# Recurrent step of a two-layer kernel: the fp32 products of update gate and candidate move from VectorE to GpSimd, and the candidate's tanh to SBUF

## Chip, cores and metric

One core of a Trainium2 chip (trn2). The metric is the device time of one execution in microseconds (us); the runs of the kernel before have a median of 7208.16 us.

## The reference, cut to what matters

Layer 0 (a gated transform of x by a small network on `cond`) is cheap here. Layer 1 is a gated recurrent unit over 2048 steps, with batch 2 and width 512, and its steps depend on each other:

```
def step(h, xs):
    xzt, xrt, xht = xs
    z = jax.nn.sigmoid(xzt + h @ U_z + vz)
    r = jax.nn.sigmoid(xrt + h @ U_r + vr)
    hh = jnp.tanh(xht + r * h @ U + vh)
    h_new = (1.0 - z) * h + z * hh
    return (h_new, h_new)
```

The kernel returns x plus these outputs. The products of x with W_z, W_r and W don't depend on h.

## The kernel before, in words

**Layout.** The width of 512 is K = 4 chunks of P = 128 partitions; batch is B = 2, so a state tile is 128 x 8 (S = 8) and half of it is 128 x 4 (HS = 4). Each fp32 factor of a product with U is split in two fp16 parts (PARTS = 2). `h_part` holds for each chunk four fp16 parts: high and low of the kept share (1-z)h and high and low of the new share z*hh. `rh_part` holds the two parts of r*h.

**One step on TensorE** (`steps`, L270, products in `tile_product`, L261). It waits for `hs0` and runs the first 16 matmuls of the reset gate into `pair_r` (input chunks 0 and 1), waits for `hs1` and runs the other 16 (chunks 2 and 3). Then 32 matmuls of the update gate into `ps_z`, and 32 of the candidate into `pair_h`, after `rh0` and `rh1`. The candidate comes in two halves, each with its own PSUM bank. After it, in four of five steps, a piece of the next block's input projection runs (`ps_p`, L238), which doesn't depend on h.

**VectorE** (`step`, L498) sums the parts of each product (`total`, L495), builds r*h (L504, L508, L513), the kept share (L532, L533, L537) and the new share. The new share has three operations per half: `new_high` (L542) rounds z_mul times tanh to fp16 in `h_part`; `new_full` (L546) computes the same product in fp32 as `zn`; `new_low` (L551) subtracts the one from the other and increments `hs0` or `hs1`. L563 then adds `keep` and `zn` to `h_cur`.

**ScalarE** does the tanh of each sum (L359), the copies that turn tanh into z_keep and z_mul (L376, L377), and the seeds: copies of the precomputed input share `xp` into the PSUM banks as one more addend (L342, L345). The tanh of the candidate's halves is written into its own bank in PSUM. Before it seeds `pair_h`, ScalarE waits for `zn1`, as `new_full` reads that bank.

**GpSimd** has only the setup (L188 to L200), and no instruction in the steps.

**Order.** Each engine runs its instructions in the order written; the engines are tied by semaphores, written out by hand, which count to the number of the step. The 2048 steps are 32 blocks of 64. A block begins with four steps with extra work (`turn`: transposes of x and of the output), then come 12 rounds of five steps with a projection each.

**Lines that matter**: the order of the tail of a step on VectorE (L554 to L563), L380 to L382 on ScalarE, L278 (the wait for `hs0` and `hs1`) on TensorE.

Of the kernel before, what the change touches and what calls it, by code (L numbers as in the profile page):

```python
# [1 line left out]

# [3 lines left out]
ALU = mybir.AluOpType  # L24
# [7 lines left out]
P = 128  # L32
R, Z, H = 0, 1, 2
# [4 lines left out]
def gru_kernel(nc, x, cond, W1, b1, W2, b2, W_z, U_z, C_z, b_z, W_r, U_r, C_r, b_r, W, U, C, b, out):  # L38
    B, T, D = x.shape
    K = D // P  # L40
    S = K * B
    HC = K // 2
    HS = S // 2
# [16 lines left out]
    with ExitStack() as ctx:  # L60
        def sb(name, shape, dt=F32):
            return ctx.enter_context(nc.sbuf_tensor(name, shape, dt))
# [43 lines left out]
        keep = sb("keep", [P, S])  # L106
        z_mul = sb("z_mul", [P, S])
        zn = sb("zn", [P, S])

# [3 lines left out]
        ps_r, ps_h = ([pair[:, hf, :] for hf in range(2)] for pair in (pair_r, pair_h))  # L115
        SUM, TANH = 64, 96

        def cols(bank, g, m0, m1):
# [6 lines left out]
                 "v_mm v_raw_ok v_ok umax_ok uall_ok upow scale_ok uhi u_ok w_ok "  # L125
                 "x_in x_tr y_ok y_copied proj0_mm proj0_ok wst_in proj_mm o_sum o_tr o_ev out_st "
                 "seed0 h0_ready r0_mm r1_mm z_mm z_keep h_ok h0_mm h1_mm r0_sum r1_sum z_sum h0_sum h1_sum r0_th r1_th z_th h0_th h1_th "
                 "rh32_0 rh32_1 rh0 rh1 keep_ok zn0 zn1 hs0 hs1 copied")
        s = {n: ctx.enter_context(nc.semaphore("s_" + n)) for n in names.split()}
        block = ctx.enter_context(nc.Block())  # L130

# [1 line left out]
        kb = lambda a: a.rearrange("p (k b) -> p k b", b=B)  # L133
        UG, WG, CG = (U_r, U_z, U), (W_r, W_z, W), (C_r, C_z, C)
        half = (slice(0, HS), slice(HS, S))
# [50 lines left out]
        @block.gpsimd  # L186
        def _(pool):
            nc.gpsimd.memset(ident[:, :], 0.0).then_inc(s["ident_zero"], 1)  # L188
            pool.wait_ge(s["ident_zero"], 1)
            nc.gpsimd.affine_select(out=ident[:, :], in_=ident[:, :], compare_op=ALU.not_equal, fill=1.0,  # L190
                                    base=0, pattern=[[-1, P]], channel_multiplier=1).then_inc(s["ident_ok"], 1)

            nc.gpsimd.memset(h_cur[:, :], 0.0)
            nc.gpsimd.memset(hist[:, TB:2 * TB, :], 0.0)
            nc.gpsimd.memset(y_cur[:, :, :], 0.0)
            nc.gpsimd.memset(h_part[:, 0:HC], 0.0).then_inc(s["hs0"], 1)
            nc.gpsimd.memset(h_part[:, HC:K], 0.0).then_inc(s["hs1"], 1)
            nc.gpsimd.memset(xp[:, :, TB:2 * TB, :], 0.0).then_inc(s["h0_ready"], 1)
            pool.wait_ge(s["umax_ok"], G)
            nc.gpsimd.partition_all_reduce(u_all[:, :], u_max[:, :], P, RMAX).then_inc(s["uall_ok"], 1)  # L200

        @block.tensor
        def _(pe):
# [123 lines left out]
        @block.scalar  # L327
        def _(act):
            A = nc.scalar.activation
            act.sem_inc(s["out_st"], BYTES)  # L330
            for n, nm in enumerate(("mlp1", "mlp2")):
                act.wait_ge(s[nm + "_pre"], 1)
                A(mlp_tanh[:, n, :], mlp_pre[:, n, :], ACT.Tanh, scale=0.5).then_inc(s[nm + "_th"], 1)
            act.wait_ge(s["scale_ok"], 1)
            for g in range(G):
                A(u_part[:, g, 0], u_raw[:, g], ACT.Copy, scale=u_scale[:, g:g + 1]).then_inc(s["uhi"], 1)

            def seed(banks, g, at):

                src = xp[:, g * K:(g + 1) * K, at, :]  # L340
                if g == Z:
                    return A(cols(banks, Z, 0, K)[:, :, ADDENDS[Z] - 1, :], src, ACT.Copy)  # L342
                a = ADDENDS[g]
                to = banks[:, :, 0:a * HS].rearrange("p h (m a b) -> p h m a b", a=a, b=B)
                return A(to[:, :, :, a - 1, :], src.rearrange("p (h m) b -> p h m b", h=2), ACT.Copy)  # L345

            act.wait_ge(s["h0_ready"], 1)
            act.wait_ge(s["proj0_ok"], 2 * G)
            for g, banks in ((R, pair_r), (Z, ps_z), (H, pair_h)):
                seed(banks, g, 0).then_inc(s["seed0"], 1)  # L350


            scale_reg = [act.alloc_register(f"tanh_scale_{g}") for g in range(G)]
            for g in range(G):
                act.reg_load(scale_reg[g], tanh_scale[0:1, g:g + 1].bitcast(I32))

            def tanh(to, bank, g, n, wait, t1, done):
                act.wait_ge(s[wait], t1)
                A(to, bank[:, SUM:SUM + n], ACT.Tanh, scale=scale_reg[g]).then_inc(s[done], 1)  # L359

            def steps(t0, count, ring, turn=None):

                for u in range(count):
                    t1 = act.snap(t0 + (u + 1))

                    prv = act.snap(ring + (u - 1) if u else (ring + (2 * TB - 1)) % (2 * TB))
                    nxt = act.snap(ring + (u + 1) if u < count - 1 else (ring + count) % (2 * TB))
                    for hf in range(2):
                        tanh(ps_r[hf][:, TANH:TANH + HS], ps_r[hf], R, HS, f"r{hf}_sum", t1, f"r{hf}_th")

                    A(hist[:, prv, :], h_cur[:, :], ACT.Copy)  # L371
                    tanh(th_z[:, :], ps_z, Z, S, "z_sum", t1, "z_th")

                    seed(pair_r, R, nxt)
                    act.wait_ge(s["z_th"], t1)
                    A(z_keep[:, :], th_z[:, :], ACT.Copy, scale=-0.5, bias=0.5).then_inc(s["z_keep"], 1)  # L376
                    A(z_mul[:, :], th_z[:, :], ACT.Copy, scale=H_SCALE / 2, bias=H_SCALE / 2)  # L377
                    tanh(ps_h[0][:, TANH:TANH + HS], ps_h[0], H, HS, "h0_sum", t1, "h0_th")
                    seed(ps_z, Z, nxt)
                    tanh(ps_h[1][:, TANH:TANH + HS], ps_h[1], H, HS, "h1_sum", t1, "h1_th")  # L380
                    act.wait_ge(s["zn1"], t1)
                    seed(pair_h, H, nxt)  # L382
                    if turn is not None and u == 1:
                        act.wait_ge(s["o_sum"], turn)
                        A(y_cur[:, :, :], y_next[:, :, :], ACT.Copy).then_inc(s["y_copied"], 1)
                    if turn is not None and u == 2:
                        put_out(turn)

            def put_out(nb):
                act.wait_ge(s["o_tr"], nb)  # L390
                act.wait_ge(s["out_st"], nb * BYTES if isinstance(nb, int) else act.snap(nb * BYTES))
                A(o_tok[:, :], ps_o[:, :], ACT.Copy).then_inc(s["o_ev"], 1)

            with act.Fori(0, NB) as n:
                steps(act.snap(n * TB), TURN, act.snap((n % 2) * TB), act.snap(n + 1))
                with act.Fori(0, GM) as i:
                    steps(act.snap(n * TB + i * BODY + TURN), BODY, act.snap((n % 2) * TB + i * BODY + TURN))
            act.wait_ge(s["h_ok"], T)
            A(hist[:, (T - 1) % (2 * TB), :], h_cur[:, :], ACT.Copy).then_inc(s["copied"], 1)
            put_out(NB + 1)  # L400

        @block.vector
        def _(dve):
            V = nc.vector
# [93 lines left out]
            def step(t1):  # L498
# [41 lines left out]
                def new_high(hf):  # L540
                    dve.wait_ge(s[f"h{hf}_th"], t1)
                    V.tensor_tensor(h_part[:, kc[hf], NEW, :], kb(z_mul[:, half[hf]]),  # L542
                                    kb(ps_h[hf][:, TANH:TANH + HS]), ALU.mult)

                def new_full(hf):
                    V.tensor_tensor(zn[:, half[hf]], z_mul[:, half[hf]], ps_h[hf][:, TANH:TANH + HS],  # L546
                                    ALU.mult).then_inc(s[f"zn{hf}"], 1)

                def new_low(hf):
                    dve.wait_ge(s[f"zn{hf}"], t1)  # L550
                    V.tensor_tensor(h_part[:, kc[hf], NEW + 1, :], kb(zn[:, half[hf]]), h_part[:, kc[hf], NEW, :],  # L551
                                    ALU.subtract).then_inc(s[f"hs{hf}"], 1)

                new_high(0)  # L554
                dve.wait_ge(s["h1_mm"], t1)
                total(ps_h[1], H, HC, "h1_sum")
                new_full(0)
                keep_low()
                new_low(0)
                new_high(1)  # L560
                new_full(1)
                new_low(1)
                V.tensor_tensor(h_cur[:, :], keep[:, :], zn[:, :], ALU.add).then_inc(s["h_ok"], 1)  # L563

# [12 lines left out]
            def steps(t0, count, proj=None, turn=None):  # L577


                for u in range(count):  # L580
                    step(dve.snap(t0 + (u + 1)))
                    if proj is not None and u == K - 1:
                        store_projection(*proj)
                    if turn is not None and u == 0:

                        make_out(turn[0])
                    if turn is not None and u == 2:
                        dve.wait_ge(s["y_copied"], turn[1])
                        make_y(turn[2])
# [35 lines left out]
```

## Time and profile before

| | |
|---|---|
| runs, median (lowest to highest) | 7208.16 us (7206.21 to 7209.48), 3 runs |
| profiled execution, span from first to last instruction | 7205.8 us |
| setup, to the first step | 74.5 us |
| busy share PE, DVE, ACT, POOL | 94%, 74%, 46%, 0% |
| instructions PE, DVE, ACT, POOL | 200232, 43503, 22603, 13 |
| granted TensorE clock, mean | 0.502 |

The profile gives the span of its execution and no separate time beside it. PE is TensorE's matmuls, PEld its weight loads, DVE is VectorE, ACT ScalarE, POOL GpSimd. The ends of matmuls are modelled, so a row of 32 matmuls may reach past the start of the next row: what counts is the distance of starts. In a timeline a row holds the start in us from the beginning of the span, the duration in us, engine, line, operation, result and operands, and the count of instructions; what stands in brackets is the idle time of the engine ahead of it and what ended it. The row of a VectorE or ScalarE operation is longer than the distance to the next independent one on its engine: they overlap.

### The profile page before, as it was taken

How to read it: one execution, taken by the hardware profiler on the slowest of the kernel's cores; microseconds unless marked ns; L12 is line 12 of the kernel's file. 1: busy time of each engine (PE TensorE's matmuls, PEld its weight loads, DVE VectorE, ACT ScalarE, POOL GpSimd, SP SyncE). 2: the span in 40 equal slices, each digit the busy share in tenths (PEclk: the TensorE clock that was granted, in tenths of full speed). 3: DMA queues.
4: the chain of work that ended last, by engine and by line, in shares of the span. 5: the costliest groups of instructions: out<-in, count | busy, mean ns of one | idle time of the engine just before them, and what ended most of it. 6: DMA issues, size and time to landing. Idle time of an engine off the chain costs nothing.

```text
span 7205.8 us, 488208 instructions
## 1 busy us (share of the span) xinstructions
PE 6775.3 (94%) x200232; PEld 6365.3 (88%) x200232; DVE 5331.0 (74%) x43503; ACT 3314.3 (46%) x22603; POOL 3.5 (0%) x13
## 2 busy tenths in 40 slices
PE   8999999999999999999999999999999999999999
PEld 7889888898888988888988889888898888988888
DVE  5777777777777777777777777777777777777777
ACT  3444444444444444444444444444444444444444
POOL 0000000000000000000000000000000000000000
PEclk5555555555555555555555555555555555555555
DMA  2000000000000000000000000000000000000000
GB/s 80 17 18 16 17 18 18 18 15 18 17 18 17 15 18 18 17 18 14 19 17 18 17 16 16 18 17 18 17 16 17 18 17 18 15 18 17 18 17 16
DMA packets 80595, 134.55 MB, mean 19 GB/s; under 512 B 12336, under 2 KB 18480, under 8 KB 80304
## 3 DMA queue, kind: packets, MB, share of 16 engines
q1 hardware_dynamic: 80304, 129.81, 5.2%
q8 instruction: 288, 4.72, 0.3%
q14 instruction: 3, 0.02, 0.0%
HBM read 20.46 MB, written 8.65 MB: 4 GB/s over the span
## 4 chain that ended last, share of the span: by engine, by line
PE 81%; DVE 12%; issue 4%; ACT 3%; SPq 0%; DMA 0%; ACTq 0%; DVEq 0%
PE pair_r L264 26%; PE pair_h L264 21%; PE ps_z L264 19%; PE ps_p L238 14%; DVE pair_r L495 2%; DVE rh_part L504 2%; DVE rh_part L513 1%; DVE h_part L532 1%; ACT pair_r L345 1%; DVE h_part L551 1%; DVE ps_z L495 1%; DVE rh L508 1%; ACT z_keep L376 1%; DVE h_part L542 1%; DVE pair_h L495 1%
## 5 line engine op out<-in xcount | busy, mean ns | idle before, releaser
L264 PEld LDWEIGHTS pair_r<-h_part,u_part 128*128 128x128 f16 x65536 | 1920.2, 105 | 755.2 <-DVE h_part L551 633.7
L264 PE MATMUL pair_r<-h_part,u_part 128*128 128x8 f16 x65536 | 2086.7, 168 | 353.3 <-DVE h_part L551 240.0
L264 PE MATMUL pair_h<-rh_part,u_part 128*128 128x4 f16 x65536 | 2186.1, 167 | 7.5 <-DVE rh_part L513 7.5
L264 PE MATMUL ps_z<-h_part,u_part 128*128 128x8 f16 x65536 | 2041.2, 168 | 42.5 <-issue 42.5
L264 PEld LDWEIGHTS pair_h<-rh_part,u_part 128*128 128x128 f16 x65536 | 2017.1, 105 | 11.0 <-DVE rh_part L513 10.2
L264 PEld LDWEIGHTS ps_z<-h_part,u_part 128*128 128x128 f16 x65536 | 1908.6, 104 | 44.5 <-issue 44.5
L495 DVE TENSOR_REDUCE pair_r<-pair_r 128x4 f32<-128x20 f32 x4096 | 757.8, 186 | 839.5 <-PE pair_r L264 792.5
L359 ACT ACTIVATE pair_r<-pair_r 128x4 f32<-128x4 f32 x4096 | 644.2, 158 | 1465.9 <-DVE pair_r L495 1360.5
L495 DVE TENSOR_REDUCE pair_h<-pair_h 128x4 f32<-128x12 f32 x4096 | 717.4, 175 | 648.6 <-PE pair_h L264 648.6
L238 PE MATMUL ps_p<-y_next,w_stage 128*128 128x128 f32 x3072 | 1189.2, 491 | 0.0
L359 ACT ACTIVATE th_z<-ps_z 128x8 f32<-128x8 f32 x2048 | 364.1, 178 | 1169.7 <-DVE ps_z L495 1169.7
L359 ACT ACTIVATE pair_h<-pair_h 128x4 f32<-128x4 f32 x4096 | 647.0, 158 | 391.5 <-DVE pair_h L495 391.0
L238 PEld LDWEIGHTS ps_p<-y_next,w_stage 128*128 128x128 f32 x3072 | 772.6, 312 | 0.0
L345 ACT ACTIVATE pair_h<-xp 128x8 f32 (+1 forms) x2049 | 370.4, 181 | 787.9 <-DVE zn L546 787.9
L551 DVE TENSOR_TENSOR h_part<-zn,h_part 128x4 f16<-128x4 f32 x4096 | 670.9, 164 | 70.7
L513 DVE TENSOR_TENSOR rh_part<-rh,rh_part 128x4 f16<-128x4 f32 x4096 | 645.9, 158 | 70.7
L504 DVE SCALAR_TENSOR_TENSOR rh_part<-pair_r,h_cur 128x4 f16<-128x4 f32 x4096 | 665.5, 163 | 34.7
L542 DVE TENSOR_TENSOR h_part<-z_mul,pair_h 128x4 f16<-128x4 f32 x4096 | 651.9, 159 | 1.3
L508 DVE SCALAR_TENSOR_TENSOR rh<-pair_r,h_cur 128x4 f32<-128x4 f32 x4096 | 627.1, 153 | 0.0
L546 DVE TENSOR_TENSOR zn<-z_mul,pair_h 128x4 f32<-128x4 f32 x4096 | 619.0, 151 | 0.0
L495 DVE TENSOR_REDUCE ps_z<-ps_z 128x8 f32<-128x40 f32 x2048 | 425.4, 208 | 45.1 <-PE ps_z L264 45.1
L371 ACT ACTIVATE hist<-h_cur 128x8 f32 x2048 | 427.6, 209 | 4.2
(70 smaller groups left out, 3315.4 us busy)
## 6 DMA issues: line engine op xcount, KB each, us to landing
w_stage<-w_in SPq DMA_DIRECT2D x384, 256.0 KB, 2.3
x_tok<-in_x SPq DMA_DIRECT2D x68, 128.0 KB, 2.6
out_dram<-o_tok SPq DMA_DIRECT2D x66, 128.0 KB, 2.4
mlp_w<-in_L_cond_W SPq DMA_DIRECT2D x2, 1024.0 KB, 6.7
u_raw<-in_L_cond_U_r SPq DMA_DIRECT2D x1, 1024.0 KB, 5.9
u_raw<-in_L_cond_U_z SPq DMA_DIRECT2D x1, 1024.0 KB, 8.0
u_raw<-in_L_cond_U SPq DMA_DIRECT2D x1, 1024.0 KB, 10.4
w_in<-in_L_cond_W_r SPq DMA_DIRECT2D x4, 256.0 KB, 9.8
```

What stands on the lines that cost most here:

```text
L238: return nc.tensor.matmul(bank[:, col:col + P], weight[:, k, :], y_next[:, k * B:(k + 1) * B, :].rearrange("p b t -> p (b t)"), start=(k = ...
L264: last = nc.tensor.matmul(cols(bank, g, m, m + 1)[:, 0, 0:ADDENDS[g] - 1, :].rearrange("p a b -> p (a b)"), u_part[:, g, part, k, gm * P:( ...
L345: return A(to[:, :, :, a - 1, :], src.rearrange("p (h m) b -> p h m b", h=2), ACT.Copy)
L359: A(to, bank[:, SUM:SUM + n], ACT.Tanh, scale=scale_reg[g]).then_inc(s[done], 1)
L371: A(hist[:, prv, :], h_cur[:, :], ACT.Copy)
L495: return V.tensor_reduce(bank[:, SUM:SUM + m * B].rearrange("p (m b) -> p m b", b=B), cols(bank, g, 0, m).rearrange("p m a b -> p m b a"), ...
L504: V.scalar_tensor_tensor(rh_part[:, kc[hf], 0, :], kb(ps_r[hf][:, TANH:TANH + HS]), 1.0, kb(h_cur[:, half[hf]]), ALU.add, ALU.mult)
L508: V.scalar_tensor_tensor(rh[:, half[hf]], ps_r[hf][:, TANH:TANH + HS], 1.0, h_cur[:, half[hf]], ALU.add, ALU.mult).then_inc(s[f"rh32_{hf}" ...
L513: V.tensor_tensor(rh_part[:, kc[hf], 1, :], kb(rh[:, half[hf]]), rh_part[:, kc[hf], 0, :], ALU.subtract).then_inc(s[f"rh{hf}"], 1)
L542: V.tensor_tensor(h_part[:, kc[hf], NEW, :], kb(z_mul[:, half[hf]]), kb(ps_h[hf][:, TANH:TANH + HS]), ALU.mult)
L546: V.tensor_tensor(zn[:, half[hf]], z_mul[:, half[hf]], ps_h[hf][:, TANH:TANH + HS], ALU.mult).then_inc(s[f"zn{hf}"], 1)
L551: V.tensor_tensor(h_part[:, kc[hf], NEW + 1, :], kb(zn[:, half[hf]]), h_part[:, kc[hf], NEW, :], ALU.subtract).then_inc(s[f"hs{hf}"], 1)
```

## The change

A tile `th_h` in SBUF takes both halves of the candidate's tanh, in place of the PSUM banks. `new_full` goes from VectorE; GpSimd computes the same fp32 product of `z_mul` and `th_h` into `zn`, for each half as soon as `h0_th` or `h1_th` is up, in a loop of 256 rounds of eight steps. `new_low` on VectorE now waits for `zn0` or `zn1` from GpSimd and for a new semaphore `zh0` or `zh1` of `new_high`. ScalarE no longer waits for `zn1` before it seeds `pair_h`. Blank lines at the head of the file go, too.

```diff
+        th_h = sb("th_h", [P, S])
@@ gpsimd, after the setup
+            def steps(t0, count):
+                for u in range(count):
+                    t1 = pool.snap(t0 + (u + 1))
+
+                    for hf in range(2):
+                        pool.wait_ge(s[f"h{hf}_th"], t1)
+                        nc.gpsimd.tensor_tensor(zn[:, half[hf]], z_mul[:, half[hf]], th_h[:, half[hf]],
+                                                ALU.mult).then_inc(s[f"zn{hf}"], 1)
+
+            with pool.Fori(0, T // 8) as n:
+                steps(pool.snap(n * 8), 8)
@@ scalar, steps
-                    tanh(ps_h[0][:, TANH:TANH + HS], ps_h[0], H, HS, "h0_sum", t1, "h0_th")
+                    tanh(th_h[:, half[0]], ps_h[0], H, HS, "h0_sum", t1, "h0_th")
                     seed(ps_z, Z, nxt)
-                    tanh(ps_h[1][:, TANH:TANH + HS], ps_h[1], H, HS, "h1_sum", t1, "h1_th")
-                    act.wait_ge(s["zn1"], t1)
+                    tanh(th_h[:, half[1]], ps_h[1], H, HS, "h1_sum", t1, "h1_th")
                     seed(pair_h, H, nxt)
@@ vector, step
                 def new_high(hf):
                     dve.wait_ge(s[f"h{hf}_th"], t1)
                     V.tensor_tensor(h_part[:, kc[hf], NEW, :], kb(z_mul[:, half[hf]]),
-                                    kb(ps_h[hf][:, TANH:TANH + HS]), ALU.mult)
-
-                def new_full(hf):
-                    V.tensor_tensor(zn[:, half[hf]], z_mul[:, half[hf]], ps_h[hf][:, TANH:TANH + HS],
-                                    ALU.mult).then_inc(s[f"zn{hf}"], 1)
+                                    kb(th_h[:, half[hf]]), ALU.mult).then_inc(s[f"zh{hf}"], 1)
 
                 def new_low(hf):
+                    dve.wait_ge(s[f"zh{hf}"], t1)
                     dve.wait_ge(s[f"zn{hf}"], t1)
@@
                 new_high(0)
                 dve.wait_ge(s["h1_mm"], t1)
                 total(ps_h[1], H, HC, "h1_sum")
-                new_full(0)
                 keep_low()
                 new_low(0)
                 new_high(1)
-                new_full(1)
                 new_low(1)
```

## Rows read from the trace of the kernel before

**Rows 1.** Section 1 of the page: busy us, share of the span, instructions.
```profile
PE 6775.3 (94%) x200232; PEld 6365.3 (88%) x200232; DVE 5331.0 (74%) x43503; ACT 3314.3 (46%) x22603; POOL 3.5 (0%) x13
```

**Rows 2.** Waits of the whole span: us in total, times, longest.
```profile
PEld pair_r L264 <- DVE h_part L551: 633.7, 1952, 0.7
PE pair_r L264 <- DVE h_part L551: 240.0, 416, 0.6
```

**Rows 3.** Timeline of one step and the next one's start, PE and PEld.
```profile
3004.34 1.07 PE L264 MATMUL pair_h<-rh_part,u_part 128*128 128x4 f16 x32
3005.27 0.77 PE L238 MATMUL ps_p<-y_next,w_stage 128*128 128x128 f32 x2
3005.98 0.93 PEld L264 LDWEIGHTS pair_r<-h_part,u_part 128*128 128x128 f16 x32 [0.23 <-DVE h_part L551]
3005.99 1.02 PE L264 MATMUL pair_r<-h_part,u_part 128*128 128x8 f16 x32
3006.87 0.99 PE L264 MATMUL ps_z<-h_part,u_part 128*128 128x8 f16 x32
3007.74 1.07 PE L264 MATMUL pair_h<-rh_part,u_part 128*128 128x4 f16 x32
```

**Rows 4.** The same step's tail: timeline, DVE and ACT.
```profile
3005.24 0.16 ACT L359 ACTIVATE pair_h<-pair_h 128x4 f32<-128x4 f32 x1
3005.43 0.16 DVE L542 TENSOR_TENSOR h_part<-z_mul,pair_h 128x4 f16<-128x4 f32 x1
3005.50 0.17 DVE L495 TENSOR_REDUCE pair_h<-pair_h 128x4 f32<-128x12 f32 x1
3005.58 0.15 DVE L546 TENSOR_TENSOR zn<-z_mul,pair_h 128x4 f32<-128x4 f32 x1
3005.65 0.16 DVE L537 TENSOR_TENSOR h_part<-keep,h_part 128x8 f16<-128x8 f32 x1
3005.71 0.16 ACT L359 ACTIVATE pair_h<-pair_h 128x4 f32<-128x4 f32 x1 [0.19 <-DVE pair_h L495]
3005.77 0.16 DVE L551 TENSOR_TENSOR h_part<-zn,h_part 128x4 f16<-128x4 f32 x1
3005.90 0.16 DVE L542 TENSOR_TENSOR h_part<-z_mul,pair_h 128x4 f16<-128x4 f32 x1
3005.97 0.15 DVE L546 TENSOR_TENSOR zn<-z_mul,pair_h 128x4 f32<-128x4 f32 x1
3006.16 0.16 DVE L551 TENSOR_TENSOR h_part<-zn,h_part 128x4 f16<-128x4 f32 x1
3006.25 0.18 ACT L345 ACTIVATE pair_h<-xp 128x8 f32 x1 [0.38 <-DVE zn L546]
3007.05 0.37 ACT L359 ACTIVATE pair_r<-pair_r 128x4 f32<-128x4 f32 x2 [0.62 <-DVE pair_r L495]
3007.53 0.15 DVE L513 TENSOR_TENSOR rh_part<-rh,rh_part 128x4 f16<-128x4 f32 x1
```

**Rows 5.** Groups by form, ACT copies: count, busy us, mean ns, idle before.
```profile
L376 ACT ACTIVATE z_keep<-th_z 128x8 f32<-128x8 f32 x2048 | 393.5, 192 | 0.0
L345 ACT ACTIVATE pair_r<-xp 128x8 f32 x2048 | 370.0, 181 | 0.0
```

**Rows 6.** Timeline of the setup: GpSimd and its neighbours.
```profile
12.55 0.28 POOL L190 TENSOR_SCALAR_AFFINE_SELECT ident<-ident 128x128 f32<-128x128 f32 x1 [11.61 <-issue]
12.88 1.11 PE L208 MATMUL ps_x<-ident,mlp_w 128*128 128x128 f32 x4 [12.88 <-POOL ident L190]
13.30 0.51 POOL L195 MEMSET y_cur<- 128x512 f32 x1
13.81 0.10 POOL L197 MEMSET h_part<- 128x16 f16 x1
13.85 1.37 POOL L198 MEMSET xp<- 128x1536 f32 x1
24.91 4.47 DVE L432 TENSOR_REDUCE u_max<-u_raw 128x1 f32<-128x2048 f32 x2
29.52 0.39 POOL L200 PARTITION_ALL_REDUCE u_all<-u_max  x1 [14.30 <-DVE u_max L432]
```

**Rows 7.** PE timeline of the start of a block.
```profile
296.11 1.01 PE L264 MATMUL pair_r<-h_part,u_part 128*128 128x8 f16 x32 [3.75 <-issue]
```

**Rows 8.** Cores: span and mean granted TensorE clock.
```profile
core 0: 7205.8 us, clock 0.502
```

More of the change, by code:

```diff
@@ L127, in gru_kernel @@
                  "seed0 h0_ready r0_mm r1_mm z_mm z_keep h_ok h0_mm h1_mm r0_sum r1_sum z_sum h0_sum h1_sum r0_th r1_th z_th h0_th h1_th "
-                 "rh32_0 rh32_1 rh0 rh1 keep_ok zn0 zn1 hs0 hs1 copied")
+                 "rh32_0 rh32_1 zh0 zh1 rh0 rh1 keep_ok zn0 zn1 hs0 hs1 copied")
         s = {n: ctx.enter_context(nc.semaphore("s_" + n)) for n in names.split()}
```

## The prediction

> **What bounds the kernel now.** I read the busy line first: PE 94%, DVE 74%, GpSimd nothing [rows 1]. By that line TensorE is the bound and work taken from VectorE would be worth nothing. But PE's ends are modelled, so I went to the waits. TensorE's weight loads for the reset gate sat idle 1952 times until `new_low` (L551) had released them [rows 2]. 1952 is 61 of the 64 steps of each of the 32 blocks. PE itself shows that wait only 416 times, in steps without a projection, where nothing fills the gap.
>
> The timeline of one step shows why both agree. The candidate's matmuls start at 3004.34, the projection at 3005.27, the next reset gate at 3005.99 and the next candidate at 3007.74: one step is 7.74 - 4.34 = 3.40 us [rows 3] (I drop the 3000 from here on). It has two parts. From the reset gate's start to the candidate's, 1.75 us, TensorE issues 64 matmuls without a pause, while the chain through r*h arrives at just the same time (L513 starts at 7.53, and 0.21 later the candidate starts) [rows 3, 4]. From the candidate's start to the next reset gate's, 1.65 us, is latency: sum, tanh, new share, `hs0`. The weight loads were idle 0.23 us ahead of 5.98 [rows 3], so the projection fills that stretch and doesn't bound it.
>
> The tail, by starts: tanh of half 0 at 5.24, `new_high` 5.43, sum of half 1 at 5.50, `new_full` 5.58, `keep_low` 5.65, `new_low` 5.77; half 1 has its tanh at 5.71, `new_high` 5.90, `new_full` 5.97, `new_low` 6.16 [rows 4]. **Hops between engines** are short: L551 starts at 5.77, is 0.16 long and PE starts at 5.99, 0.06 behind its end; tanh ends at 5.40 and L542 starts at 5.43 [rows 3, 4].
>
> `hs0` sets TensorE's start. `hs1` has little slack: the second 16 matmuls are due half of 6.87 - 5.99 = 0.88 us behind the start, at 6.43, and `hs1` is seen 0.22 behind L551's start, at 6.38. Slack 0.05 us [rows 3, 4].
>
> **The change part by part.** *Removed from VectorE:* two products per step. Each took a slot of some 0.07 us between starts. The first one does nothing for the critical time by itself: `new_low` at 5.77 stood 0.19 behind the start of the product whose semaphore it waits for (5.58), and not behind `keep_low` (5.65 + 0.07 = 5.72) [rows 4]. What matters is when `zn` is there. *Removed from ScalarE:* the wait of 0.38 us before the seed of `pair_h` at 6.25. ScalarE's next work on the chain is the tanh of the reset gate at 7.05, for which it idled 0.62 us [rows 4]. Worth nothing; the cover is that idle time.
>
> *Tanh to SBUF.* The trace has no PSUM-to-SBUF tanh of 4 columns. A copy of 8 columns from SBUF takes 192 ns with its result in SBUF and 181 ns with it in PSUM [rows 5]: +0.01 us each. Half 1 pays twice, as its sum queues behind `new_high(0)`. Bounds: 0 and 0.02. `new_high` reading SBUF in place of PSUM I set at nothing: L542 and L551 take 0.16 us each, though the one reads PSUM and the other SBUF [rows 4]. The Trainium skill, Perfetto Trace Analysis, section "Optimizing Scalar/DVE Operations", puts a ScalarE access at some 93 ns on SBUF and 51 on PSUM: by an estimate from that page the tanh would be 0.04 us longer, not 0.01, and the forecast some 60 us higher for half 0's share alone. The rows of copies here speak for the small figure.
>
> *Added on GpSimd:* the path from tanh's end over GpSimd to `new_low`'s start, which I call L. Three terms:
> - the hop in. L432 ends at 24.91 + 4.47 = 29.38 and L200 starts at 29.52: 0.14 us. Lower bound 0.03, the hop from ScalarE to VectorE above [rows 4, 6].
> - the product itself, 128x4 with two operands read. No such row exists. Memsets of 512 and 1536 columns take 0.51 and 1.37 us: 0.84 ns per column. The affine select of 128 columns reads one operand: 0.28 - 128 x 0.00084 = 0.17 us fixed. A memset of 16 columns is 0.10 [rows 6], so reading one operand adds about 0.07; for the second I take half of that or a little more. 0.22 us. Bounds: 0.10 (the memset) and 0.39 (the all-reduce, the longest row of fixed cost).
> - the hop out: L190 ends at 12.83, PE starts at 12.88: 0.05 us [rows 6].
>
> L = 0.14 + 0.22 + 0.05 = 0.41 us, between 0.18 and 0.58. Before, it was 5.77 - 5.40 = 0.37 with nothing from another engine in it.
>
> *Half 0:* tanh ends 5.41, `new_low` at 5.82, 0.05 later than before. *Half 1:* tanh ends 5.89, `new_low` at 6.30, seen at 6.52, against 6.43: 0.14 late minus 0.05 slack, 0.09; with rounding of the stamps I take **0.08 us per step**. Half 1 decides, as its start waits on nothing that half 0 gives back. The new wait stands in VectorE's queue: behind `new_low(0)` wait `new_high(1)`, due at 5.91 and now at 5.82 + 0.07 = 5.89 at the earliest, so it isn't late; behind `new_low(1)` waits L563 alone, whose result is wanted a microsecond later. `zh0` and `zh1` come 0.19 behind `new_high`, at 5.63 and 6.10, ahead of `zn`: free. No DMA is moved or added, and GpSimd's queue had nothing in the steps to be moved past.
>
> *The sum:* the shift is paid in the 61 of 64 steps in which L551 releases TensorE. Of the others one waits 3.75 us for issue [rows 7] and the two behind transposes have cover. 1952 x 0.08 = 156 us. 7205.8 + 156 = 7362; the median of the runs stands 2.4 us above the span, inside my error. Forecast **7360 us**.
>
> **The rivals.**
> *GpSimd is quick (faster), 0.20.* Place: `zn1` at `new_low(1)`. It decides at L = 6.43 - 0.22 - 5.89 = 0.32: below that neither half is late. With the low bounds, L = 0.18, VectorE's own order is next: `new_low(0)` at 5.50 + 0.08 + 0.07 = 5.65 or 5.66, 0.11 sooner, and `new_low(1)` at 6.10 behind `zh1`, seen 6.32, just when its matmuls are due (5.88 + 0.44). 1952 x 0.11 = 215: 6990 us. For it speaks that small GpSimd memsets start 0.04 us apart [rows 6]; against it that they read nothing. With L near 0.28 it gives 0.04 x 1952 = 80, so 7130.
>
> *GpSimd and VectorE get in each other's way (slower), 0.20.* `new_high` now reads both inputs from SBUF at the very time when GpSimd reads the same two tiles, and `keep_low` reads two inputs from SBUF right behind it. If each holds the other off for the rest of a row: GpSimd starts behind `new_high`'s end, 5.44 + 0.16 = 5.60 in place of 5.55; its product ends at 5.82; `keep_low` waits for that and `new_low(0)` starts at 5.89, +0.12. Half 1: `new_high` 5.92 to 6.08, product to 6.30, `new_low(1)` at 6.35, seen 6.57, while the second half is due at 6.11 + 0.44 = 6.55. 0.14 x 1952 = 273: 7480 us. No row of this trace shows two such operations side by side. The Trainium skill, SBUF — State Buffer, section "Who interferes with whom", says so as a rule: a VectorE instruction with two SBUF inputs contends with a GpSimd instruction that reads SBUF, and the later one blocks. That no trace here can yet bear out.
>
> *A GpSimd product costs like the all-reduce, 0.12.* L = 0.58; half 1 is seen at 5.89 + 0.58 + 0.22 = 6.69, +0.26: 507 us, 7710 us.
>
> *GpSimd's loop stalls, 0.05.* TensorE stalls 3.75 us where its block begins [rows 7]. GpSimd is free from 6.25 to the next tanh's end at 8.81, 2.56 us, so such a stall at each of its 256 loop ends would show 1.2 us: 305 us over the forecast, 7665 us.
>
> *The hop and product come out at the old 0.37 less the slack, 0.05:* within 0.2% of 7208, which is about what a measurement of this kernel can tell from no change.
>
> **How the numbers follow.** Forecast 0.38, quick GpSimd 0.20, mutual blocking 0.20, slow product 0.12, loop 0.05, no change 0.05. Faster 0.20, same 0.05, slower 0.75. The range runs from 7130 (the milder half of the quick case) to 7700, which leaves about 0.1 on either side. The forecast's own range, with the product between 0.18 and 0.28, is 7280 to 7480.
>
> **What would show it right or wrong.** A GpSimd row of 0.22 us that starts 0.14 behind the tanh's end; L551 at 0.41 behind that end in both halves; weight loads idle 0.31 in place of 0.23 us ahead of the reset gate; a step of 3.48 us; ScalarE's seed of `pair_h` right behind the second tanh. It is wrong if L is under 0.32, or if `keep_low` or `new_high` grow or start late, which would be the blocking, or if the gaps sit at one step in eight, which would be the loop. TensorE's granted clock stands at the lower of its levels, 1.2 GHz (mean 0.502 [rows 8]), and I count on no change there, as TensorE only gets idler.

## The result and the profile after

The changed kernel takes 7416.3 us (median of 4 runs, 7414.8 to 7420.4) against 7207.2 us of the kernel before, a ratio of 1.029 (1.0275 to 1.0304): 209 us slower. That lies in the stated range; the forecast had 153 us. The direction was right and so was the place, but one term of the sum came out right by luck, from wrong parts, as the experiments show.

Sections 1 and 5 of the page after, beside [rows 1] of before (VectorE's lines have moved: `new_high` is L536, `new_low` L542, the sums L489):

```profile
PE 6968.0 (94%) x200232; PEld 6504.4 (88%) x200232; DVE 5214.6 (70%) x39407; ACT 3196.5 (43%) x22603; POOL 829.8 (11%) x4109
L191 POOL TENSOR_TENSOR zn<-z_mul,th_h 128x4 f32<-128x4 f32 x4096 | 826.3, 202 | 6551.0 <-ACT th_h L354 6551.0
L354 ACT ACTIVATE th_h<-pair_h 128x4 f32<-128x4 f32 x4096 | 710.6, 173 | 433.6 <-DVE pair_h L489 433.2
```

VectorE lost 4096 instructions and 116 us of busy time, and none of it came off the span. TensorE's share is 94% as before: it is spread over a longer time because its modelled rows grow where it pauses between matmuls. The waits of after, beside [rows 2]:

```profile
PEld pair_r L259 <- DVE h_part L542: 680.2, 1952, 0.7
DVE h_part L542 <- POOL zn L191: 378.2, 2048, 0.2
```

The same 1952 steps wait for `hs0`, by only 47 us more in total (0.024 each). The timeline of one step, PE, ACT, GpSimd and VectorE, beside [rows 3, 4], tells the rest:

```profile
3001.09 1.07 PE L259 MATMUL pair_h<-rh_part,u_part 128*128 128x4 f16 x32
3001.99 0.17 ACT L354 ACTIVATE th_h<-pair_h 128x4 f32<-128x4 f32 x1
3002.20 0.17 DVE L536 TENSOR_TENSOR h_part<-z_mul,th_h 128x4 f16<-128x4 f32 x1
3002.24 0.20 POOL L191 TENSOR_TENSOR zn<-z_mul,th_h 128x4 f32<-128x4 f32 x1 [2.80 <-ACT th_h L354]
3002.48 0.17 ACT L354 ACTIVATE th_h<-pair_h 128x4 f32<-128x4 f32 x1 [0.21 <-DVE pair_h L489]
3002.55 0.16 DVE L542 TENSOR_TENSOR h_part<-zn,h_part 128x4 f16<-128x4 f32 x1
3002.69 0.17 DVE L536 TENSOR_TENSOR h_part<-z_mul,th_h 128x4 f16<-128x4 f32 x1
3002.73 0.20 POOL L191 TENSOR_TENSOR zn<-z_mul,th_h 128x4 f32<-128x4 f32 x1 [0.29 <-ACT th_h L354]
3002.77 1.08 PE L259 MATMUL pair_r<-h_part,u_part 128*128 128x8 f16 x32
3003.04 0.17 DVE L542 TENSOR_TENSOR h_part<-zn,h_part 128x4 f16<-128x4 f32 x1 [0.18 <-POOL zn L191]
3003.71 0.99 PE L259 MATMUL ps_z<-h_part,u_part 128*128 128x8 f16 x32
3004.58 1.07 PE L259 MATMUL pair_h<-rh_part,u_part 128*128 128x4 f16 x32
```

The step is 4.58 - 1.09 = 3.49 us, 0.09 longer. Behind the first tanh's start, `new_low(0)` comes at 0.56 (before 5.77 - 5.24 = 0.53) and `new_low(1)` at 1.05 (before 0.92) [rows 4]. So TensorE starts 0.03 later and then pauses in mid-gate for `hs1`: from its start to the update gate's it takes 0.94 us in place of 0.88, its row 1.08 in place of 1.02 [rows 3]. 0.03 + 0.06 = 0.09. The second part is in no wait of TensorE's list; it hides in the length of a row of 32. Looked at in windows of 0.1 us, that row has 10 matmuls in the one from 3003.10 and 7 in the one from 3003.20, where the second 16 are due (2.77 + 0.44 = 3.21); the row of the kernel before keeps 10 or 11 in each from 3006.20 to 3006.70.

1952 x 0.09 = 176 us. The rest sits at one step in five:

```profile
3010.09 0.16 DVE L552 TENSOR_TENSOR h_cur<-keep,zn 128x8 f32<-128x8 f32 x1
3010.54 0.29 DVE L557 TENSOR_TENSOR xp<-ps_p,v_bias 128x128 f32 x1 [0.29 <-issue]
3010.75 0.30 DVE L489 TENSOR_REDUCE pair_r<-pair_r 128x4 f32<-128x20 f32 x2
```

The projection's store (`store_projection`) starts 0.45 behind `h_cur`. TensorE began this gate at 3009.74, so the first sum was due 0.90 later, at 3010.64, as in the step above (3003.67 - 3002.77); it starts at 3010.75, 0.11 late, and the candidates of this step stand 3.56 us apart (3008.07 and 3011.63), not 3.49. In the kernel before, the same rows, beside a gate that began at 3016.19:

```profile
3016.44 0.16 DVE L563 TENSOR_TENSOR h_cur<-keep,zn 128x8 f32<-128x8 f32 x1
3016.84 0.29 DVE L568 TENSOR_TENSOR xp<-ps_p,v_bias 128x128 f32 x1 [0.24 <-issue]
3017.05 0.38 DVE L495 TENSOR_REDUCE pair_r<-pair_r 128x4 f32<-128x20 f32 x2
```

The first sum stood 0.86 behind the gate's start there (0.84 in a step without the store) and stands 1.01 behind it now: 0.10 because `h_cur` follows TensorE's start by 0.35 in place of 0.25, and 0.05 because the store starts 0.45 and not 0.40 behind `h_cur`. 384 x 0.07 = 27 us. Together 203 of the 209, the rest being within the rounding of the stamps (0.005 x 1952 = 10 us).

### The profile page after: what moved, and what is told of

The parts are those of the page before. It is cut to its first block, busy times and chain, and to the rows that moved or that the text cites. A ratio compares the mean times of both kernels' runs of the same rounds, so it can differ in the third digit from the quotient of the medians.

```text
span 7414.8 us, 495377 instructions
## 1 busy us (share of the span) xinstructions
PE 6968.0 (94%) x200232; PEld 6504.4 (88%) x200232; DVE 5214.6 (70%) x39407; ACT 3196.5 (43%) x22603; POOL 829.8 (11%) x4109
## 4 chain that ended last, share of the span: by engine, by line
PE 88%; DVE 6%; issue 4%; ACT 1%; POOL 0%; SPq 0%; DMA 0%; DVEq 0%; POOLq 0%
PE pair_r L259 28%; PE pair_h L259 23%; PE ps_z L259 22%; PE ps_p L233 13%; DVE pair_h L489 1%; DVE h_part L542 1%; DVE h_part L536 1%; DVE h_part L526 1%; PE ps_o L203 0%; DVE keep L527 0%; POOL zn L191 0%; DVE rh_part L498 0%; DVE h_part L531 0%; DVE rh_part L507 0%; DVE pair_r L489 0%
## 5 line engine op out<-in xcount | busy, mean ns | idle before, releaser
L259 PEld LDWEIGHTS pair_r<-h_part,u_part 128*128 128x128 f16 x65536 | 2042.6, 105 | 801.3 <-DVE h_part L542 680.2
L259 PE MATMUL pair_r<-h_part,u_part 128*128 128x8 f16 x65536 | 2209.4, 169 | 362.1 <-DVE h_part L542 249.6
L191 POOL TENSOR_TENSOR zn<-z_mul,th_h 128x4 f32<-128x4 f32 x4096 | 826.3, 202 | 6551.0 <-ACT th_h L354 6551.0
L489 DVE TENSOR_REDUCE pair_r<-pair_r 128x4 f32<-128x20 f32 x4096 | 732.0, 186 | 734.3 <-PE pair_r L259 693.1
L489 DVE TENSOR_REDUCE pair_h<-pair_h 128x4 f32<-128x12 f32 x4096 | 718.1, 175 | 665.6 <-PE pair_h L259 665.6
L542 DVE TENSOR_TENSOR h_part<-zn,h_part 128x4 f16<-128x4 f32 x4096 | 675.5, 165 | 442.9 <-POOL zn L191 378.2
L354 ACT ACTIVATE th_h<-pair_h 128x4 f32<-128x4 f32 x4096 | 710.6, 173 | 433.6 <-DVE pair_h L489 433.2
L536 DVE TENSOR_TENSOR h_part<-z_mul,th_h 128x4 f16<-128x4 f32 x4096 | 674.8, 165 | 7.3
L489 DVE TENSOR_REDUCE ps_z<-ps_z 128x8 f32<-128x40 f32 x2048 | 422.6, 206 | 49.2 <-PE ps_z L259 49.2
L372 ACT ACTIVATE z_mul<-th_z 128x8 f32<-128x8 f32 x2048 | 394.6, 193 | 0.0
```

The costliest lines, as they stand in the source:

```text
L191: nc.gpsimd.tensor_tensor(zn[:, half[hf]], z_mul[:, half[hf]], th_h[:, half[hf]], ALU.mult).then_inc(s[f"zn{hf}"], 1)
L259: last = nc.tensor.matmul(cols(bank, g, m, m + 1)[:, 0, 0:ADDENDS[g] - 1, :].rearrange("p a b -> p (a b)"), u_part[:, g, part, k, gm * P:( ...
L489: return V.tensor_reduce(bank[:, SUM:SUM + m * B].rearrange("p (m b) -> p m b", b=B), cols(bank, g, 0, m).rearrange("p m a b -> p m b a"), ...
```

## The experiments

Theory at the start: GpSimd's answer comes too late (**late hand-over**). Rivals: the place of the tanh; contention of VectorE and GpSimd at SBUF; each product on GpSimd costing alike. Each kernel's runs alternated with runs of the kernel before, and each difference is taken from those: their median was 7201.4 us beside e1 to e4, 7203.9 beside e5 to e8 and 7208.8 beside e9 to e11.

**e1: tanh in SBUF, products on VectorE.** From the kernel before:

```diff
-                    tanh(ps_h[0][:, TANH:TANH + HS], ps_h[0], H, HS, "h0_sum", t1, "h0_th")
+                    tanh(th_h[:, half[0]], ps_h[0], H, HS, "h0_sum", t1, "h0_th")
...
-                    act.wait_ge(s["zn1"], t1)
```

(the second half likewise; `new_high` and `new_full` read `th_h`)

> The tanh of the candidate goes to SBUF and ScalarE's wait for zn1 is gone, but both fp32 products stay on VectorE. Late hand-over theory (GpSimd's answer to the second half comes too late for the reset gate's second 16 matmuls): only the tanh's longer row is left, +0.02 us per step on hs0 and +0.04 on hs1, of which 0.05 is slack: 1952 x 0.02 = 39 us over the kernel before, about 7246. Rival, the place of the tanh is most of it: 7350 to 7416.

7256.9 us, ratio 1.0078 (1.0064 to 1.0092): about 55 us, somewhat over the 39. The tanh's row is 173 ns, in place of 158 with its result in PSUM, and candidates stand some 3.425 us apart. So a quarter of the loss is the tanh's new place, less whatever the removed wait of ScalarE gives, which wasn't tried by itself.

**e2 and e3: only one half's product on GpSimd.** From the changed kernel; e2 gives GpSimd half 0, e3 half 1 (with `(1,)`, and `new_full(0)` ahead of `keep_low`). The edit of e2:

```diff
-                    for hf in range(2):
+                    for hf in (0,):
                         pool.wait_ge(s[f"h{hf}_th"], t1)
...
                 new_high(1)
+                new_full(1)
                 new_low(1)
```

> Only the first half's product is on GpSimd; the second half's stays on VectorE, with the tanh in SBUF. Late hand-over theory: hs0 is 0.03 us later than in the kernel before, hs1 0.04, inside its slack: +0.03 x 1952 = 59 us, about 7266. Rival, each product on GpSimd costs alike, through contention of the two engines at SBUF: half of the 209 us, about 7311 or more, as keep_low lies beside this half's product.

> Only the second half's product is on GpSimd. Late hand-over theory: hs0 +0.02, hs1 seen 0.06 us after its matmuls are due: 0.08 x 1952 = 156 us, and 27 us more from the projection's store that is pushed behind the reset gate's sums: about 7390. Rival, each product costs alike: about 7311, and by contention less than the first half's, as no VectorE operation with two SBUF inputs lies beside it.

e2 7397.7 us, ratio 1.0273 (1.0259 to 1.0287); e3 7428.0 us, 1.0315 (1.0301 to 1.0329). Both miss, e2 by 130 us and e3 by 38, and the rival fell too: the two don't share the loss. e2 is 196 us over the kernel before and e3 227, so with only one product on GpSimd the kernel is about as slow as with both. The timeline of e2 on VectorE shows where:

```profile
3003.41 0.16 DVE L546 TENSOR_TENSOR h_part<-zn,h_part 128x4 f16<-128x4 f32 x1
3003.55 0.17 DVE L536 TENSOR_TENSOR h_part<-z_mul,th_h 128x4 f16<-128x4 f32 x1
3003.63 0.15 DVE L540 TENSOR_TENSOR zn<-z_mul,th_h 128x4 f32<-128x4 f32 x1
3003.89 0.16 DVE L546 TENSOR_TENSOR h_part<-zn,h_part 128x4 f16<-128x4 f32 x1
```

In the second half no GpSimd takes part: L540 is `new_full` on VectorE. Still `new_low` (L546) starts 0.26 behind it, where it was 0.19 in the kernel before (5.97 to 6.16 [rows 4]). It is 0.19 in e1 too, where both operations read SBUF as here:

```profile
3002.27 0.16 DVE L546 TENSOR_TENSOR zn<-z_mul,th_h 128x4 f32<-128x4 f32 x1
3002.46 0.16 DVE L551 TENSOR_TENSOR h_part<-zn,h_part 128x4 f16<-128x4 f32 x1
```

And in e3 it is half 0, whose product is on VectorE, that is late:

```profile
3001.73 0.15 DVE L540 TENSOR_TENSOR zn<-z_mul,th_h 128x4 f32<-128x4 f32 x1
3001.99 0.16 DVE L546 TENSOR_TENSOR h_part<-zn,h_part 128x4 f16<-128x4 f32 x1
```

Again 0.26. TensorE starts 0.84 behind that half's tanh, 0.09 later than before (0.03 of it the tanh's place, as in e1), and then doesn't pause for `hs1` (its row is 1.01): the whole loss of e3's steps sits at the half that GpSimd doesn't touch. What both versions of `new_low` here have and the old one hasn't is a second wait, for `zh`. With a theory of 0.07 us for it the changed kernel fits as well: GpSimd's second product ends at 2.93, and 3.04 is 0.11 behind it, where other hops took 0.03 to 0.06.

**e4: is there contention?** Two more products per step on GpSimd, on tiles of their own, one where VectorE is not reading two SBUF tiles and one beside the kept share:

```diff
+                    for sem, to in (("rh1", pr_quiet), ("z_keep", pr_busy)):
+                        pool.wait_ge(s[sem], t1)
+                        nc.gpsimd.tensor_tensor(to[:, :], pr_in[:, half[0]], pr_in[:, half[1]], ALU.mult)
```

> The changed kernel with two more GpSimd products of 128x4 per step on tiles of their own, one where VectorE has no operation with two SBUF inputs (behind rh1), one beside the kept share's two products (behind z_keep). Late hand-over theory: both rows are 0.20 us as the real ones, VectorE's rows for the kept share stay at 0.16 to 0.17, and the time is that of the changed kernel within 0.2%, 7416. Rival, contention at SBUF: the quiet product's row is 0.15 or less, and the busy one's longer, or the kept share's rows grow by 0.03 or more and the time with them (60 us for each 0.03).

7413.8 us, ratio 1.0294 (1.0278 to 1.031), the changed kernel's time. Its groups by form:

```profile
L196 POOL TENSOR_TENSOR pr_quiet<-pr_in 128x4 f32<-128x4 f32 x2048 | 406.8, 199 | 4169.0 <-DVE rh_part L515 4169.0
L196 POOL TENSOR_TENSOR pr_busy<-pr_in 128x4 f32<-128x4 f32 x2048 | 406.8, 199 | 886.9 <-ACT z_keep L379 886.9
L535 DVE TENSOR_TENSOR keep<-z_keep,h_cur 128x8 f32<-128x8 f32 x2048 | 357.4, 175 | 0.0
L534 DVE TENSOR_TENSOR h_part<-z_keep,h_cur 128x8 f16<-128x8 f32 x2048 | 345.1, 169 | 5.1
```

Quiet and busy are alike, 199 ns. One VectorE row grew: `keep` from 160 ns in the changed kernel to 175. `keep_low`, which lies beside the real product, stays at 158, and `new_high` beside it takes 165 as in e1 (165), where GpSimd does nothing. So what contention there is comes to 0.015 us on one row, not to a block of a row's length. The Trainium skill, SBUF — State Buffer, section "Who interferes with whom", says that a VectorE instruction with two SBUF inputs contends with a GpSimd instruction that reads SBUF, and calls the port pair that they share an exclusive lock. For operations of four to eight columns the trace shows 15 ns where waiting out the other's row would take up to 0.16 us or more.

**e5: the order of the two waits.** One swap in the changed kernel:

```diff
                 def new_low(hf):
-                    dve.wait_ge(s[f"zh{hf}"], t1)
                     dve.wait_ge(s[f"zn{hf}"], t1)
+                    dve.wait_ge(s[f"zh{hf}"], t1)
```

> The changed kernel with new_low's two waits in the other order: first for GpSimd's zn, then for new_high's zh. GpSimd's row ends 0.11 us before new_low starts, against 0.03 to 0.05 for other engines. Theory, the hop out of GpSimd is simply longer: no change, 7416. Rival, the first wait is an instruction of its own and its handling costs: swapping makes that one wait end last, and the time moves by 0.03 us or more per step (60 us), up if a separate wait costs more than an attached one.

7268.7 us, ratio 1.009 (1.0077 to 1.0104). Two lines in another order give back 144 of the 209 us (209 - 65). The rival was right that the waits matter and had the direction open; if a separate wait is the dear one, then it was zn's, written last, that stood by itself in the changed kernel. Its timeline:

```profile
3002.09 0.20 POOL L191 TENSOR_TENSOR zn<-z_mul,th_h 128x4 f32<-128x4 f32 x1 [2.90 <-ACT th_h L354]
3002.32 0.16 DVE L542 TENSOR_TENSOR h_part<-zn,h_part 128x4 f16<-128x4 f32 x1
3002.33 0.17 ACT L354 ACTIVATE th_h<-pair_h 128x4 f32<-128x4 f32 x1 [0.22 <-DVE pair_h L489]
3002.58 0.20 POOL L191 TENSOR_TENSOR zn<-z_mul,th_h 128x4 f32<-128x4 f32 x1 [0.29 <-ACT th_h L354]
3002.81 0.17 DVE L542 TENSOR_TENSOR h_part<-zn,h_part 128x4 f16<-128x4 f32 x1
```

`new_low` now starts 0.03 behind the end of GpSimd's product in both halves, a hop like any other. The steps without the store are 3.42 us, those with it still 3.49: the store's 0.07 isn't the order's.

**e10 and e11: the wait alone, without GpSimd.** The kernel before, all products on VectorE and in PSUM; `new_high` increments `zh`, and `new_low` waits for it ahead of `zn` (e10) or behind it (e11) in the code. e10:

```diff
                 def new_low(hf):
+                    dve.wait_ge(s[f"zh{hf}"], t1)
                     dve.wait_ge(s[f"zn{hf}"], t1)
```

> The kernel before, everything on VectorE and in PSUM as it was; only new_high increments zh and new_low waits for zh and then zn, as in the changed kernel. Theory formed from e2, e3 and e5: where new_low waits for two semaphores, the one written last in the code becomes a wait of its own ahead of the instruction, and if that one comes last it costs some 0.07 us (new_low started 0.07 behind the time when zn could be seen in the changed kernel, and 0 behind it in e5). Here zn comes last: 0.07 x 1952 = 137 us more, about 7341. Rival, the 0.07 us belong to GpSimd's hand-over: no change, 7204.

> As e10 with the two waits in the other order, so that the early zh is the wait of its own. Theory: no change, 7204 within 0.2%. Rival, any second wait costs 0.07 us: 7341.

e10 7362.9 us, ratio 1.0215 (1.0201 to 1.0229); e11 7219.7 us, 1.0016 (1.0007 to 1.0025). From e10's timeline:

```profile
3005.46 0.15 DVE L546 TENSOR_TENSOR zn<-z_mul,pair_h 128x4 f32<-128x4 f32 x1
3005.72 0.16 DVE L552 TENSOR_TENSOR h_part<-zn,h_part 128x4 f16<-128x4 f32 x1
```

and from e11's:

```profile
3003.82 0.15 DVE L546 TENSOR_TENSOR zn<-z_mul,pair_h 128x4 f32<-128x4 f32 x1
3004.01 0.16 DVE L552 TENSOR_TENSOR h_part<-zn,h_part 128x4 f16<-128x4 f32 x1
```

0.26 against 0.19. Both came out about as expected (137 us and none). A wait that asks for nothing late costs 154 us by its place in the code, and 11 us in the other order. This settles it: 0.07 us per `new_low`, with no GpSimd in the kernel. What the trace can't show is what becomes of the waits in the program. The explanation that fits is that one instruction holds one wait and the other stands ahead of it as an instruction of its own, behind whose release the next one has yet to be handed on; the Trainium skill, Perfetto Trace Analysis, section "Identifying Dependency Chains", says that further wait conditions may be put in instructions inserted ahead. The runs give the price: 0.07 us if the separate one is the last to come, and nothing on `new_low` if it comes early. The 11 us of e11 sit in steps with the projection's store (some 3.44 in place of 3.40 us; 384 x 0.04 = 15):

```profile
3004.09 0.16 DVE L564 TENSOR_TENSOR h_cur<-keep,zn 128x8 f32<-128x8 f32 x1
3004.54 0.29 DVE L569 TENSOR_TENSOR xp<-ps_p,v_bias 128x128 f32 x1 [0.29 <-issue]
```

The store starts 0.45 behind `h_cur`, 0.29 of it issue, where the kernel before has 0.40 and 0.24. It is 0.43 to 0.45 in every kernel in which `new_low(1)` has a second wait and the store stands in its old place, whatever the order (the changed kernel, e2 to e5, e10, e11), and 0.40 or 0.41 in those without (the kernel before, e1, e7, e9). So a second wait there costs the store 0.05 us even when it asks for nothing late; the runs don't show how.

**e6 and e8: the projection's store elsewhere.** In the changed kernel (e6) and in the kernel before (e8) it runs in the round's fifth step, behind the update gate's sum, and no longer behind `h_cur`:

```diff
                 total(ps_z, Z, K, "z_sum")
+                if store is not None:
+                    store_projection(*store)
```

> The changed kernel with the projection's store moved from between two steps (behind h_cur of the fourth step of a round) into the fifth step, behind the update gate's sum, where VectorE idles 0.32 us. Theory: in the changed kernel the store ends 0.07 us behind the time when the reset gate's sums could start, once per round of five, as h_cur is 0.1 us later against TensorE's start: 384 x 0.07 = 27 us come back, 7389. Rival, the store is hidden and the fifth step is longer for another reason: no change, 7416.

> The kernel before with the projection's store moved as in e6. There the store pushes the reset gate's sums by some 0.02 us only: 384 x 0.02 = 8 us, 7199, at the edge of what can be told. If the store were the 27 us in the kernel before too, 7180.

e6 7440.9 us, ratio 1.0329 (1.0315 to 1.0343); e8 7254.3 us, 1.0071 (1.0057 to 1.0084). Both got slower. The four steps of a round without the store are now all of 3.48 us in e6, so the 0.07 is the store's, as supposed. But the new place is worse: 3.63 us in e6, 3.56 in e8, which had lost nothing at the old one. From e8:

```profile
3016.54 0.21 DVE L495 TENSOR_REDUCE ps_z<-ps_z 128x8 f32<-128x40 f32 x1
3017.02 0.29 DVE L570 TENSOR_TENSOR xp<-ps_p,v_bias 128x128 f32 x1 [0.28 <-issue]
3017.23 0.17 DVE L495 TENSOR_REDUCE pair_h<-pair_h 128x4 f32<-128x12 f32 x1
```

I had counted the row against an idle 0.32 us. The store starts 0.48 behind the operation ahead of it, 0.28 of it idle for issue; that its address depends on a register may be why, but no run tried it without. With its own 0.21 until the next start it needs a hole of 0.69 us.

**e7: another product on GpSimd.** The kernel before with `keep` = z_keep * h_cur moved:

```diff
-                V.tensor_tensor(keep[:, :], z_keep[:, :], h_cur[:, :], ALU.mult).then_inc(s["keep_ok"], 1)
+                    nc.gpsimd.tensor_tensor(keep[:, :], z_keep[:, :], h_cur[:, :], ALU.mult).then_inc(s["keep_ok"], 1)
```

> The kernel before, with another fp32 product of the step on GpSimd: keep = z_keep * h_cur (128x8), whose reader keep_low is due 0.45 us behind z_keep, not 0.19 behind its product's start. Late hand-over theory: 0.08 + 0.21 + 0.11 = 0.40 us behind z_keep's end, in time for keep_low: no change, 7207 within 0.2%. Rival, any product on GpSimd costs this kernel time (contention, or the hand-over itself): +60 us or more.

7203.4 us, ratio 1.0 (0.9991 to 1.0009). An fp32 product of twice the columns moves to GpSimd for nothing when its reader isn't due. `keep_low` has two waits in it as well, the late one written last, and still the step is 3.40 us: that reader has the time.

**e9: what beats both.** Half 0 on GpSimd with `zn0` waited for first; half 1 as before:

```diff
+                    nc.gpsimd.tensor_tensor(zn[:, half[0]], z_mul[:, half[0]], th_h[:, :], ALU.mult).then_inc(s["zn0"], 1)
...
                     dve.wait_ge(s[f"zn{hf}"], t1)
+                    if hf == 0:
+                        dve.wait_ge(s["zh0"], t1)
...
-                new_full(0)
```

> A version meant to beat both: only the first half's product on GpSimd, its tanh in SBUF, new_low(0) waiting for zn0 first in the code; the second half as in the kernel before (VectorE, PSUM, one wait). Theory: new_low(0) starts 0.48 us behind its tanh's start in place of 0.53, the second half's 0.93 in place of 0.92 behind that tanh: the reset gate's matmuls start 0.05 sooner and pause 0.01 for hs1, so a step is 0.04 us shorter. 78 us less, of which the projection's store takes some 20 back: about 7145. Rival, the second half or TensorE holds the step at 3.40 us: 7204.

7189.8 us, ratio 0.9975 (0.9964 to 0.9985): 19 us faster than the kernel before, its sign as expected and its size a third of it.

```profile
3003.72 0.17 ACT L369 ACTIVATE th_h<-pair_h 128x4 f32<-128x4 f32 x1
3004.20 0.16 DVE L565 TENSOR_TENSOR h_part<-zn,h_part 128x4 f16<-128x4 f32 x1
3004.42 1.05 PE L274 MATMUL pair_r<-h_part,u_part 128*128 128x8 f16 x32
3004.66 0.16 DVE L565 TENSOR_TENSOR h_part<-zn,h_part 128x4 f16<-128x4 f32 x1
```

`new_low(0)` comes 0.48 behind the tanh, 0.05 sooner than before, and TensorE starts 0.05 sooner. `new_low(1)`, at 0.94, then holds it up in mid-gate by 0.03 (its row is 1.05 in place of 1.02). A step is 3.38 to 3.39 us, and 3.41 with the store. 0.02 x 1952 = 39 us less and 0.03 x 384 = 12 back make 27, against 19 measured, which the rounding of the stamps covers. The second half is the bound now.

## Why the prediction was right, and where not

**The bound.** Right: 1952 steps wait for `hs0`, TensorE's clock is unchanged (mean 0.502), and work off VectorE was worth nothing by itself. Half 1 decides, by `hs1` and its small slack, also right: of 0.09 us per step 0.06 is TensorE's pause in mid-gate. The slack shows across the runs: the reset gate's row is 1.01 to 1.02 us while `new_low(1)` starts 0.17 to 0.20 behind TensorE (the kernel before, e1, e3, e10), 1.05 at 0.24 (e9) and 1.08 at 0.27 (the changed kernel, e5). I had the 0.08 per step nearly right, but by luck.

**The step that failed** is the one on the new wait: "`zh0` and `zh1` come 0.19 behind `new_high`, at 5.63 and 6.10, ahead of `zn`: free". They do come ahead (`new_high` ends at 3002.37 and 3002.86, GpSimd's product at 3002.44 and 3002.93), and yet the second wait costs 0.07 us in each half by the order of two lines (e5, e10). I asked only when a semaphore arrives, not what a second wait does to the instruction. Two other terms were too high and covered the gap, so that the sum L came out within 0.02:

| term | predicted, us | measured, us |
|---|---|---|
| hop in, tanh's end 2.16 to product's start 2.24 | 0.14 | 0.08 |
| the product | 0.22 | 0.20 |
| hop out | 0.05 | 0.03 (e5) |
| order of the waits | 0 | 0.07 (e10, e11) |
| L, tanh's end to `new_low` | 0.41 | 0.39 |

The hop in was read from the all-reduce behind a VectorE operation, another kind of instruction. Without the order of the waits L is 0.31 (e5: 2.01 to 2.32), a hair under the 0.32 that I had named as the point where the quick rival decides. **That rival** was nearly right about GpSimd, and the kernel would still not have been faster: e5 is 65 us over the kernel before. With the tanh in SBUF half 1's tanh starts 0.49 behind half 0's and not 0.47, and `new_low(1)` comes at 0.97 and not 0.92, so TensorE starts 0.05 sooner and pauses 0.06.

**The tanh in SBUF.** Sized at 0.01 us per tanh from copies; its row grew by 0.015, and `new_high` started 0.21 behind the tanh's start in place of 0.19. e1 gives 55 us for it all, where two tanhs of 0.01 were worth 39 at most. The estimate of 0.04 from the Trainium skill, Perfetto Trace Analysis, section "Optimizing Scalar/DVE Operations", which I had weighed against the copies, was too high here.

**The term that was missing** is the store of the projection, 27 us. I had looked at what waits behind `new_low(1)` and found "L563 alone, whose result is wanted a microsecond later". In one step of five the store queues behind L563, and it ended just in time before. The 0.01 that was missing per step (0.09, not 0.08) is some 20 us more; the two make up most of the 56 us between forecast and result.

**Mutual blocking** fell with e4, and a **slow product** with the row of 0.20 us. **The loop's stall** fell as well: GpSimd is idle 2.79 to 2.87 us ahead of each step's first product, with nothing every eight steps, and what 0.08 there is comes with the store. The weight loads' idle time went up by 0.02 us, not the 0.08 that I had named as a sign: the other part of the delay doesn't stand ahead of the gate, but inside it.

The parts of the 209 us, along one path: about 144 the order of the waits (209 less e5's 65; e10 has 154 for the same two waits in the kernel before), about 55 the tanh's place (e1), and some 10 what is left (e5 less e1). That last part holds two things: steps without the store are 0.01 us shorter in e5 than in e1 (3.42 and 3.43), those with it 0.05 longer (3.49 and 3.44). With the order mended, GpSimd's hand-over costs about what it saves.

## What to carry to other kernels

Where an instruction waits for two semaphores on a path that bounds the kernel, try both orders of the waits: here the wait for the late one has to be written first. Moving an elementwise product to GpSimd costs some 0.31 us from one engine's end to another's start, so it is free where the reader is due later than that (e7), of use where VectorE's own order is slower (half 0 in e9), and a loss where VectorE's is quicker (half 1: `new_low` 0.48 behind its tanh's start in e5, 0.45 before). Some operations need a hole for their issue too, not only for their row: the store here starts 0.40 to 0.48 us behind whatever stands ahead of it.

## What the runs showed that I had not expected

- The order of two waits on one VectorE instruction, worth 0.07 us each time and 144 us in all (e5), and a second wait that is never late still costs the store behind it 0.05 us (e11).
- GpSimd's affine select in the setup starts at 1.17 us in the changed kernel, and at 12.55 in the kernel before, where GpSimd was idle 11.61 us ahead of it [rows 6]. It starts at 1.17 in every kernel with a GpSimd product, and at 11.5 to 12.6 in those without (the kernel before, e1, e8, e10, e11). The first step began 2.5 us sooner after the change (72.08 in place of 74.57), but over all runs it begins between 71.5 and 75.2 with either start (e4 74.55, e10 71.48), so it is worth nothing that can be told here.

```profile
1.17 0.29 POOL L173 TENSOR_SCALAR_AFFINE_SELECT ident<-ident 128x128 f32<-128x128 f32 x1 [0.24 <-POOL ident L171]
```

- A delay of TensorE in the middle of a group of matmuls shows in no wait and in no idle time at the row's start, only in the group's length (1.02 to 1.08 us).
